# A mixture-of-experts kernel: the shared expert of two token groups placed behind the routed blocks

## What is computed

```python
x1 = _ln(x) * (1.0 + scale1) + shift1           # shift, scale, gate from the condition
q, k, v = split((x1 @ qkv_w + qkv_b))           # 16 heads of 128
x = x + gate1 * (softmax(q @ k.T * scale) @ v @ out_w + out_b)
x2 = _ln(x) * (1.0 + scale2) + shift2
h = x + gate2 * (gelu(x2 @ ffn_w1 + ffn_b1) @ ffn_w2 + ffn_b2)
...
probs = softmax(h @ router_w.T)                 # 16 experts
top_vals, top_idx = top_k(probs, 4)             # normalised to sum 1
y = (silu(h @ w_gate[e]) * (h @ w_up[e])) @ w_down[e]     # experts are 176 wide
routed = sum over the four chosen of top_val * y
shared = silu(h @ sh_gate) * (h @ sh_up) @ sh_down        # 704 wide
out = x_in + routed + sigmoid(h @ sh_gate_w) * shared
```

## Time and profile before

| | us |
|---|---|
| median of 3 runs (992.02 to 997.2) | 993.25 |
| the profiled execution | 993.17 |
| its span, from the first to the last instruction | 991.4 |

### The profile page before, as it was taken

The page is one execution under the profiler, slowest core; times in us unless marked ns, Lnnn a source line. Parts: engine busy times, 40 slices in busy tenths (PEclk is TensorE's granted clock), DMA queues, the critical chain, the costliest instruction groups (busy, mean ns, idle before and its releaser), DMA issues.

```text
span 991.4 us, 17761 instructions
## 1 busy us (share of the span) xinstructions
PE 908.5 (92%) x5692; PEld 812.3 (82%) x5692; DVE 616.8 (62%) x1447; ACT 481.8 (49%) x1296; POOL 307.1 (31%) x231
## 2 busy tenths in 40 slices
PE   4899999999999999989999999999959899999950
PEld 4788988989899898979898778788848789999940
DVE  5864446454464544664465777666785777777748
ACT  2545454454554545534545555654513545555520
POOL 1330303012020120270001615666751654444430
PEclk9999999999999999999999999999979999999985
DMA  5999961010010100120002004245302433334338
GB/s 187 342 353 352 339 211 49 0 48 0 0 48 0 48 0 0 48 86 22 1 23 98 23 22 140 79 159 198 102 11 65 159 109 118 119 112 123 115 125 314
DMA packets 73043, 107.77 MB, mean 109 GB/s; under 512 B 6793, under 2 KB 61198, under 8 KB 72720
## 3 DMA queue, kind: packets, MB, share of 16 engines
q1 hardware_dynamic: 31280, 53.10, 16.4%
q10 hardware_dynamic: 34832, 36.77, 11.8%
q0 software_dynamic: 6864, 17.06, 4.6%
HBM read 50.99 MB, written 57.87 MB: 110 GB/s over the span
## 4 chain that ended last, share of the span: by engine, by line
PE 80%; DVE 14%; issue 2%; POOL 2%; DMA 1%; ACT 1%; SPq 0%; POOLq 0%; DVEq 0%; ACTq 0%
PE bank L1335 45%; PE bank L1707 8%; PE bank L1419 6%; PE bank L1398 5%; PE bank L1730 5%; PE bank L1407 3%; PE bank L1667 3%; DVE acc L1324 3%; PE bank L1693 2%; PE bank L1718 2%; DVE hid_area L846 2%; DVE work L1221 1%; DVE work L1299 1%; POOL hs L537 1%; DVE work L915 1%
## 5 line engine op out<-in xcount | busy, mean ns | idle before, releaser
L1335 PE MATMUL bank<-tok_area,arena_a 128*128 128x512 f32 x768 | 208.4, 408 | 4.9 <-DVE tok_area L846 4.4
L846 DVE TENSOR_TENSOR hid_area<-bank,hid_area 128x256 fp32r<-128x256 f32 (+2 forms) x222 | 110.8, 499 | 114.9 <-ACT hid_area L627 107.2
L1335 PEld LDWEIGHTS bank<-tok_area,arena_a 128*128 128x128 f32 x768 | 139.4, 192 | 30.4 <-DVE tok_area L846 4.8
L612 ACT ACTIVATE work<-bank,negm 128x128 f32<-128x128 f32 x256 | 90.5, 367 | 92.3 <-DVE negm L908 92.2
L605 ACT ACTIVATE work<-bank,bqk_sb 128x512 f32<-128x512 f32 x128 | 88.2, 689 | 74.9 <-PE bank L1335 74.9
L1335 PE MATMUL bank<-arena_a,tok_area 128*128 128x256 f32 x768 | 108.6, 291 | 0.0
L371 POOL TENSOR_TENSOR arena_a<-raw,fixed 128x1536 fp32r<-128x1536 f32 x7 | 19.2, 2747 | 274.8 <-DMA bv_sb<-in_bv 274.8
L549 POOL DMA_INDIRECT ys<-work,dest x79 | 76.9, 973 | 86.4 <-DVE dest L1303 80.5
L1707 PE MATMUL bank<-wE,hid_area 128*128 x474 | 98.3, 343 | 5.1 <-DVE hid_area L846 5.1
L1335 PEld LDWEIGHTS bank<-arena_a,tok_area 128*128 128x128 f32 x768 | 97.0, 193 | 0.0
L1335 PE MATMUL bank<-hid_area,x_area 128*128 128x512 f32 x384 | 96.1, 399 | 0.0
(11 more groups left out here) (160 smaller groups left out, 1596.5 us busy)
## 6 DMA issues: line engine op xcount, KB each, us to landing
hs<-h_even ACTq DMA_DIRECT2D x1, 35904.0 KB, 119.1
work<-hs SPq DMA_DIRECT2D x79, 132.0 KB
we_raw<-in_we SPq DMA_DIRECT2D x16, 608.0 KB, 5.6
y_all<-ys SPq DMA_DIRECT2D x8, 1024.0 KB, 12.1
raw<-in_wqkv SPq DMA_DIRECT2D x8, 768.0 KB, 4.4
work<-in_x SPq DMA_DIRECT2D x4, 512.0 KB, 6.3
raw<-in_wo SPq DMA_DIRECT2D x8, 256.0 KB, 4.3
raw<-in_w SPq DMA_DIRECT2D x2, 1024.0 KB, 5.9
```

Source lines behind the costliest of these rows:

```text
L612: last = nc.scalar.activation(probs[:, m, i], SC_BANK[m][:, i * T:i * T + T], ACT.Exp, bias=negm[:, m, i:i + 1], scale=SCALE, accum_out=rs ...
L846: return nc.vector.tensor_tensor(target, whole, high.bitcast(f32), ALU.subtract)
L1335: last = nc.tensor.matmul(out_ap, stationary(s), moving(m), start=start and i == 0, stop=stop and i == len(PARTS) - 1)
```

## The change

The shared expert of token groups 0 and 1 (`FRONT` = 12 chunks) stays ahead of the blocks; that of groups 2 and 3 comes after the last block. The 12 late chunks have a second copy of the shared weights and of the two groups' h, loaded into the space of the first experts from block 64 on (by ScalarE's queue) and split into halves again (`late_high` on ScalarE, `late_low` on GpSimd: three parts beside blocks 70, 72 and 74, five behind the blocks). For this SP stores h of groups 2 and 3 to DRAM (`h_kept`), and `make_h` waits for the store.

The weights of a token's four choices travel in the payload (12 columns instead of 8): `slots` finds them, `destinations` sums out weight and destination together, and `keep_y` scales each block's result by it. At the end GpSimd adds the four results in pairs (`s_pair`), and VectorE adds the two pair sums to `acc_tok` (`add_results`), one piece q behind each of the late chunks 3 to 10.

The router's work is done some steps earlier, and for the last group it takes chunks 0 to 9 instead of 0 to 17. The experts are loaded in another order; expert 11 is loaded and split beside the feed-forward part; VectorE makes the low half of four experts (two in chunks 10 and 11, two beside blocks 3 and 7), GpSimd of twelve (five between the third and the fourth group's scatters, where it had four). The rings of block rows and of block results have eight places.

```diff
+FRONT_G = 2
+FRONT = FRONT_G * SC
-RING = 7
+RING = 8
+Y_RING = 8
+EARLY = 11
+LOW_V = (6, 8, 9, 13)
+FIRST = (0, 1, 2, 3, 4)
+LOW_P = (EARLY, 0, 1, 2, 3, 4, 5, 7, 10, 12, 14, 15)
-PAY = 8
+PAY = 3 * TOPK
...
+        LATE = (("w", 0), ("h", 0), ("w", 1), ("w", 2), ("w", 3), ("w", 4), ("w", 5), ("h", 1))
```

On SP:

```diff
+            for g in range(FRONT_G, TG - 1):
+                keep_rows(g)
             sp.wait_ge(s_ff_down, TG)
-            for e in range(0, 3):
+            for e in FIRST[0:3]:
                 load_expert(e)
+            keep_rows(TG - 1)
+            for e in (3, 4, 7, 6):
+                load_expert(e)
...
             for i in range(RING):
                 load_block(i)
-            sp.wait_ge(s_sh_down, SHARED)
-            for e in range(11, E):
+            sp.wait_ge(s_gate_up[0], FRONT)
+            sp.wait_ge(s_gate_up[1], ups(FRONT))
+            for e in (9, 10):
+                load_expert(e)
+            sp.wait_ge(s_sh_down, FRONT)
+            for e in range(12, E):
                 load_expert(e)
```

On GpSimd:

```diff
-            scatter(0, 0, 10)
+            low_expert(EARLY)
+            scatter(0, 0, 6)
             own = inverse_root(TG + 3, 1, own)
-            scatter(0, 10, 16)
+            scatter(0, 6, 16)
             scatter(1, 0, 16)
             scatter(2, 0, 16)
-            for e in range(0, 4):
+            for e in FIRST:
                 low_expert(e)
             scatter(3, 0, 16)
-            for e in range(4, 13):
+            rest_of = LOW_P[1 + len(FIRST):]
+            for e in rest_of[0:2]:
                 low_expert(e)
             for i in range(BLOCKS):
                 scatter_y(i)
-                if i < 3:
-                    low_expert(13 + i)
+                if i < 2 * len(rest_of[2:]) and i % 2 == 0:
+                    low_expert(rest_of[2 + i // 2])
+                if i in (70, 72, 74):
+                    late_low((i - 70) // 2)
+            for n in range(3, len(LATE)):
+                late_low(n)
+            for q in range(B // 2):
+                pool.wait_ge(s_y4_loaded[q], 16)
+                for k in (0, 2):
+                    two = y4[:, 2 * q:2 * q + 2]
+                    pool.tensor_tensor(two[:, :, k], two[:, :, k], two[:, :, k + 1], ALU.add).then_inc(s_pair, 1)
```

On ScalarE:

```diff
+            early = {1: (0, 1), 2: (2, 3), 3: (4,), 5: (5,), 6: (6,), 7: (7,), 8: (8,)}
+            for i in range(FRONT):
                 shared_silu(i)
                 shared_high(i)
                 if i == 0:
-                    high_h(TG - 1)
+                    exponentials(TG - 1)
                 if i == 1:
-                    exponentials(TG - 1)
-                if i == 2:
                     keep_h(TG - 1)
+                for e in early.get(i, ()):
+                    high_expert(e)
...
-                nc.scalar.activation(y_blk[i % 3], Y_B[i % 2][:, 0:D], ACT.Copy).then_inc(s_y_kept, 1)
+                nc.scalar.activation(y_blk[i % Y_RING], Y_B[i % 2][:, 0:D], ACT.Copy, scale=sum_b[i % 4][:, 1:2])\
+                    .then_inc(s_y_kept, 1)
...
+            shared_silu(FRONT)
             keep_y(BLOCKS - 1)
+            late_high(3)
+            shared_high(FRONT)
+            for i in range(FRONT + 1, SHARED):
+                shared_silu(i)
+                if 4 + i - FRONT - 1 < len(LATE):
+                    late_high(4 + i - FRONT - 1)
+                shared_high(i)
```

On VectorE:

```diff
+                own = step(nc.vector.tensor_tensor(match, key.unsqueeze(2).to_broadcast(four),
+                                                   top2[:, :, 0:TOPK].unsqueeze(3).to_broadcast(four), ALU.is_equal), own + 1)
+                own = step(nc.vector.tensor_tensor(match, match, comb[:, some, 0:E].unsqueeze(2).to_broadcast(four),
+                                                   ALU.mult), own)
...
+                nc.vector.tensor_reduce(h_tok[r % 2][:, :, D + 2 * TOPK:HROW], match, AX.X, ALU.add).then_inc(s_slots, 1)
...
-                        if c == 7:
+                        if c == (4 if last_g else 6):
                             own = slots(g - 1, own)
...
+            for i in range(FRONT):
                 shared_gated_up(i)
                 shared_low(i)
...
                 if i == 1:
-                    low_h(TG - 1)
+                    own = probabilities(TG - 1, own)
+                    own = largest(own)
                 if i == 2:
-                    own = probabilities(TG - 1, own)
+                    own = shares(TG - 1, own)
                 if i == 3:
-                    own = largest(own)
+                    own = slots(TG - 1, own)
                 if i == 4:
-                    own = shares(TG - 1, own)
+                    own = ranges(own)
...
+                if i >= 10:
+                    low_expert(LOW_V[i - 10])
...
+                if i in (3, 7):
+                    low_expert(LOW_V[2 + i // 4])
+
+            def add_results(q, own):
+                here = acc_tok[:, 2 * q:2 * q + 2]
+                dve.wait_ge(s_pair, 2 * q + 1)
+                dve.wait_ge(s_sh_kept, BG * (FRONT_G + (q == 5)))
+                own = step(nc.vector.tensor_tensor(here, here, y4[:, 2 * q:2 * q + 2, 0], ALU.add), own)
+                dve.wait_ge(s_pair, 2 * q + 2)
+                nc.vector.tensor_tensor(here, here, y4[:, 2 * q:2 * q + 2, 2], ALU.add).then_inc(s_summed, 1)
+                return own
+
+            for i in range(FRONT, SHARED):
+                shared_gated_up(i)
+                shared_low(i)
+                if FRONT + 3 <= i < FRONT + 3 + B // 2:
+                    own = add_results(i - FRONT - 3, own)
+                if i == FRONT + SC:
+                    keep_shared(FRONT_G)
+            keep_shared(TG - 1)
```

On TensorE:

```diff
-                        if c == 6:
+                        if c == (3 if g == TG - 1 else 5):
                             positions(g - 1)
...
+                if late and i <= FRONT + SC:
+                    pe.wait_ge(s_late_split, i - FRONT + 2)
...
+            shared_gate_up(FRONT)
             block_down(BLOCKS - 1, behind)
+            shared_gate_up(FRONT + 1)
+            for i in range(FRONT, SHARED):
+                if i + 2 < SHARED:
+                    shared_gate_up(i + 2)
+                shared_down(i)
```

292 lines of the change are left out of this document (176 added, 116 removed).

## The result

| | us |
|---|---|
| median after (982.65 to 991.23, 5 runs) | 986.37 |
| median before, beside it (5 runs) | 993.25 |
| ratio, with its 95% interval | 0.9933 [0.9908, 0.9959] |
| the profiled execution after, and its span | 982.65, 980.7 |

The change gains 0.7% where 1.4% were forecast. The same kernel was timed once more beside the experiments: 983.09 us (9 runs) against 992.43, ratio 0.9908 [0.9884, 0.9932], a gain of 0.9%. The sign and the places of the gain are as forecast; the prices were too low, and one rule on which they rested is wrong.

What follows compares the result with a forecast made beforehand. It took the kernel as TensorE work plus holes, the largest at the end. Span 991.4 - 32.2 - 13.5 + 12 + 2 + 3 + 15 = 977.7, plus 1.8 gives 979.5 us; own range 966 to 988, stated range 957 to 997.

Steps and rivals of the forecast that it cites:

- the term of 12 us: Ahead of the blocks: twelve chunks covering the last group's routing, with VectorE held by GpSimd subtractions; +12 us, bounds 0 to 20.
- the term of 15: Late shared chunks behind the last block: TensorE waits for VectorE, held up by GpSimd's work; +15 us, bounds 5 to 20.
- the tail: End of the kernel: late chunks cover the results' return, leaving some 4.5 us after the last matmul instead of 36.7; -32.2 us.
- the stall of `ranges`: Shared expert ahead of the blocks: the 16-column tensor_scalar moves away from five subtractions, ending idle and half-clock time; -13.5 us.
- the feed-forward part: Earlier, longer `slots` of groups 0 and 1 delays TensorE 1.3 us each time; +2 us, bounds -1 to 4.
- The blocks: Routed blocks: GpSimd and VectorE subtractions beside early blocks and 70, 72, 74 cost time; +3 us, bounds -3 to 7.
- the wait (a): Behind the blocks: VectorE's first add waits for GpSimd's last split and first pair sum; TensorE stalls 5.4 us.
- The hold-ups (b): Behind the blocks: sixteen pair sums delay three VectorE operations a chunk; 2.4 us lost each, full price 12, 9 taken.
- the rule under "What takes its place ahead of the blocks": Front shared chunks: the tensor_scalar of `shares` waits through a string of four subtractions, 10.9 us; 5 taken for TensorE.
- the two splits in chunks 10 and 11: Front shared chunks: VectorE takes over two subtractions, with GpSimd's own two beside them; 2 us, between 0 and 4.
- rival 3: Slower: two-operand VectorE instructions shut out for a whole string, sixteen pair sums standing bare behind the blocks; 1003.5 us, chance 0.08.
- Rival 1: Every VectorE operation waits for one GpSimd instruction only; ahead +4, behind +5, others 0; 956.5 us, chance 0.22.

Runs made afterwards that it cites:

- joined kernel: Against the change: four adds on VectorE without GpSimd sums, two splits waiting for the last front low half, slots of groups 0 and 1 put back; 975.65 us, ratio 0.9822.

## Why the prediction came out as it did

The step that failed is the price of VectorE beside GpSimd's strings. Ahead of the blocks the term of 12 us measured some 14 (16.5 in the second profile), and behind them the term of 15 measured 17.8 (18.3); the rule for who gets in was wrong ahead of the blocks, the size was off behind them. The terms of the tail, of `ranges` and of the feed-forward part held.

**Right: the tail.** TensorE's last matmul ends 4.4 us from the end (forecast 4.5; 36.7 in the earlier trace rows), and the return lies beside chunks. **Right: the stall of `ranges`**, 13.70 us to 0.18; nothing of that kind took its place at that line. **Right: the feed-forward part**: two waits of 1.91 and 1.89 us where the earlier trace rows had 0.67, together 2.5 more (forecast 2); put back, the joined kernel's idle there falls by the same 2.5. **The blocks** cost 1 us net (forecast 3, bounds -3 to 7). TensorE didn't wait for the first rows.

**Mis-sized: behind the blocks**, forecast 15, measured about 17.8 (the stage against 47.4 us of chunks and its end). By the rows: the wait (a) 3.88 us, forecast 5.4, and 1.6 us of half clock on the gate behind it (4.58 against 3.0), for which the sum had next to nothing: 5.5. The hold-ups (b) 0.41 + 1.72 + 4.35, and 1.3 + 1.0 us at half clock behind the last (2.90 against 1.60, 3.89 against 2.9): 8.8, forecast 9 of 12. The period of VectorE's chunk is the 6.4 us of the sum (936.61 to 943.01). What the sum had not seen is the 1.41 us for the first of GpSimd's late splits behind the blocks, ahead of F + 2, and 0.68 at the last low half. That is 16.4 of the 17.8; the rest stands in no single wait. Taking the sums away, with VectorE's sixteen adds left as they were, gave 13 us back, which shows that the cause of the price is the one named: GpSimd's string and the wait for its first sum.

**Wrong: the rule under "What takes its place ahead of the blocks".** There a tensor_scalar was to wait for a whole string of subtractions, and by the part on the late stage a two-operand instruction gets in behind one. The price, 12, came out as some 14.3 (10.9 us of idle and about 5 at half clock are in the rows, of which some 1.7 stood there before too, beside the stall of `ranges`), but its parts were other ones. `shares`, for which its tensor_scalar was to be held 5 to 11 us, got in after 2.08 (TensorE 1.00 and 2.94 us, forecast 5); `slots` cost 1.19 (forecast 4); and the two splits in chunks 10 and 11, priced at 2, cost 3.87 and half clock behind it, because there a two-operand low half was kept out to the end of the string. That the total is off by 2.3 only is in part luck: `shares` and `slots` together took 3.9 us of idle less than forecast, the splits more. The experiments have it out to the end of four, seven and fourteen instructions (9.81, 18.73, 19.71 us). So the mechanism of rival 3 exists, though not at the sums, where the rival put it: there VectorE got in at every boundary.

Rival 1, with one instruction as the longest wait, would have given 956.5 us. The Trainium skill (SBUF — State Buffer, "Who interferes with whom") has the lock last one whole instruction and go to whoever issues first. The 18.73 us speak against that as a bound on the wait: after the first subtraction six more, issued later, went ahead of VectorE.

**Not in the sum: the level of the profiled execution.** The forecast added 1.8 us to the span, as the profiled execution before stood at its median. That of after was the shortest of its five, 3.7 us below theirs. The mark of the first shared gate, behind code that none of the experiments but the joined ones changes, lies between 656.4 and 662.3 us in their profiles; a difference of 3 us between two single executions need not be an effect of a change. So by the first profile 3.0 of the 6.9 us by which 979.5 missed the median are prices, and the rest is this. The split isn't firm: in the second profile (span 982.4) the same terms miss by 4.5 ahead of the blocks and 3.3 behind them, with 1.0 and 2.1 less than forecast in the blocks and before the shared expert, 4.7 together; and the median of the second series, 983.09, is missed by 3.6 only. That the first series lay higher is chance as far as these runs show.

**What stays open** is who gets in between two GpSimd instructions that are both ready. Kind of VectorE's operation, length, operand pattern and place in the string have fallen. Nor does it suffice to ask whether GpSimd's next input was ready before VectorE came: it was where VectorE was held 5.25 and 18.73 us and at the earlier trace rows, but also at the sums, which let it in each time. Not tried is what else sets the sums apart, which overwrite one of their inputs; it can't be the whole rule, as the subtractions alone do both (2.08 us in the change, 9.81 in the joined kernels).

## What to carry to other kernels

A VectorE operation with two SBUF operands, or a tensor_scalar, beside a string of ready GpSimd instructions waited here for one of them or for the whole string, and no rule told which: give both prices, and let a critical one not meet such a string; a wait that breaks the string pays only if it doesn't delay what stands behind it in GpSimd's queue (scatters, the next expert's half). Where a stage is made shorter, look at what the next one loads at a fixed time: the blocks gave back half of 6 us, as the loads of two experts didn't come sooner. Where work is laid beside a stage to be covered, add up each engine's chain for one step of that stage, its waits for the other engines included: the cover was long enough for the return (47 us against 34), yet VectorE's step of 6.4, then 4.8 us against TensorE's 4.2 was the bound. And a job that lies beside another engine's wait of 0.7 us a step is free there: moving one of four equal adds into it, with `keep_shared` ahead of its adds, made the stage 3.8 us shorter.

## What the runs showed of the hardware

Fourteen short GpSimd instructions kept one VectorE operation out as long as seven long ones (19.71 and 18.73 us). While GpSimd's sums ran and VectorE got in between them, both paid: the sum that followed took 1.7 us instead of 1.26, VectorE's add 1.7 instead of 0.68. And TensorE's granted clock was at the lower of its two levels, 1.2 GHz, behind the idle stretches of 2.94, 3.87, 3.88 and 4.35 us in the two shared stretches of after: the twelve matmuls of a down-projection took 2.93 us behind 3.87 us of idle and 1.60 elsewhere, so this stall cost 1.3 us more than its idle time in that row alone.
